# A transformer decoder layer on one core: idle products, an earlier bias product, roots before masked picks and bf16 mask rows in its first rounds

## What is computed

```python
x = x + self_attention(layernorm(x), W_qkv)          # causal, scale 1/sqrt(128)
q, k, v = layernorm(x) @ Wq.T + bq, ctx @ Wk.T + bk, ctx @ Wv.T + bv    # 16 heads of 8
scores = where(mask == 0, -1e9, q @ k.T / sqrt(8))   # mask: 32 x 1 x 128, int32
x = x + (softmax(scores) @ v) @ Wo.T + bo
g, u = qdq(h @ Wg.T), qdq(h @ Wu.T)                  # h = qdq(layernorm(x)), qdq: 16-bit levels
x = x + qdq(qdq(g * u16(sigmoid(g))) * u) @ Wd.T
```

## Time and profile before

| what | us |
|---|---|
| median of three runs (332.31 to 333.15) | 332.85 |
| the profiled execution | 332.82 |
| its span, first to last instruction | 331.0 |
| TensorE busy | 304.9 (92%) |
| VectorE busy | 273.5 (83%) |
| ScalarE busy | 255.1 (77%) |
| GpSimd busy | 192.1 (58%) |
| DMA, mean over the span | 69 GB/s |

### The profile page before, as it was taken

The page is one execution under the profiler, slowest core; times in us unless marked ns, Lnnn a source line. Parts: engine busy times, 40 slices in busy tenths (PEclk is TensorE's granted clock), DMA queues, the critical chain, the costliest instruction groups (busy, mean ns, idle before and its releaser), DMA issues.

```text
span 331.0 us, 9933 instructions
## 1 busy us (share of the span) xinstructions
PE 304.9 (92%) x3741; PEld 208.7 (63%) x3741; DVE 273.5 (83%) x652; ACT 255.1 (77%) x470; POOL 192.1 (58%) x339
## 2 busy tenths in 40 slices
PE   2899999999999999999999999999978689697996
PEld 1587877877656666666666665854423244357996
DVE  5349998878979999999999984877789996989754
ACT  3258988887789989989988987787797768993940
POOL 3467999984238698768658578200067773781000
PEclk9999999999999999999999999999997999999999
DMA  6891336672011556500000000000000000000134
GB/s 155 248 300 35 96 110 184 190 219 95 30 42 49 176 160 191 170 4 5 3 5 2 4 5 2 1 0 0 2 0 0 1 1 2 0 0 1 34 95 128
DMA packets 23755, 22.70 MB, mean 69 GB/s; under 512 B 3546, under 2 KB 21403, under 8 KB 23579
## 3 DMA queue, kind: packets, MB, share of 16 engines
q1 hardware_dynamic: 22170, 21.78, 21.4%
q10 hardware_dynamic: 1536, 0.28, 0.5%
HBM read 15.75 MB, written 6.31 MB: 67 GB/s over the span
## 4 chain that ended last, share of the span: by engine, by line
PE 65%; DVE 12%; ACT 8%; POOL 7%; issue 4%; DMA 2%; SPq 1%; POOLq 0%; ACTq 0%; DVEq 0%
PE banks L763 11%; PE banks L707 9%; PE banks L989 8%; DVE mxs L1820 7%; PE banks L1059 7%; PE banks L637 5%; PE banks L785 4%; PE banks L776 3%; PE banks L630 3%; ACT ng L1355 2%; PE banks L781 2%; PE banks L716 2%; POOL rstd L380 2%; PE banks L649 2%; PE banks L971 2%
## 5 line engine op out<-in xcount | busy, mean ns | idle before, releaser
L1594 DVE TENSOR_REDUCE nm<-banks 128x4 f32<-128x512 f32 x128 | 83.1, 682 | 7.2 <-PE banks L707 5.8
L1258 ACT ACTIVATE PT<-banks,bmask,vmask 128x1024 f32<-128x1024 f32 x64 | 76.6, 1199 | 0.0
L989 PE MATMUL banks<-X3T,upT 128*128 128x512 f32 x96 | 45.9, 620 | 9.9 <-DVE mxs L1820 7.3
L576 POOL TENSOR_TENSOR G<-ng,sq 128x1536 int32<-128x1536 int32 (+3 forms) x10 | 27.9, 2790 | 36.4 <-DVE sq L1851 36.4
L1820 DVE TENSOR_REDUCE mxs<-G 128x1 f32<-128x1536 int32 (+3 forms) x30 | 42.2, 1425 | 4.3 <-ACT G L1316 3.8
L763 PE MATMUL banks<-PT,VP 128*32 128x128 f32 x1024 | 41.2, 279 | 0.0
L989 PEld LDWEIGHTS banks<-X3T,upT 128*128 128x128 f32 x96 | 17.7, 196 | 33.8 <-issue 16.3
L707 PE MATMUL banks<-kd,qd 32*128 32x128 f16 x512 | 37.9, 217 | 1.1 <-ACT pT L1130 0.7
L1100 ACT ACTIVATE h<-X,shift,rstd 128x128 f32<-128x128 f32 x64 | 26.3, 483 | 10.2 <-POOL shift L425 10.1
L707 PEld LDWEIGHTS banks<-kd,qd 32*128 32x128 f16 x512 | 22.7, 92 | 17.7 <-DVE nm L1594 7.2
L763 PEld LDWEIGHTS banks<-PT,VP 128*32 128x32 f32 x1024 | 24.1, 109 | 9.8 <-issue 3.0
(11 more groups left out here) (200 smaller groups left out, 744.4 us busy)
## 6 DMA issues: line engine op xcount, KB each, us to landing
kd<-k_dram SPq DMA_DIRECT2D x32, 128.0 KB, 2.7
qd<-q_dram SPq DMA_DIRECT2D x32, 128.0 KB, 2.8
ctxg<-in_ctx_dram SPq DMA_DIRECT2D x8, 256.0 KB, 3.1
X3T<-m_dram SPq DMA_DIRECT2D x1, 1792.0 KB, 10.2
out_dram<-y SPq DMA_DIRECT2D x7, 256.0 KB, 2.3
X<-in_x_dram SPq DMA_DIRECT2D x3, 512.0 KB, 10.0
k_dram<-khi SPq DMA_DIRECT2D x7, 128.0 KB, 1.9
k_dram<-klo SPq DMA_DIRECT2D x7, 128.0 KB, 1.9
```

Of the source, the lines that this page charges most:

```text
L576: nc.gpsimd.tensor_tensor(GI[:, c], ng[:, u, part], sq[:, u, part], ALU.mult).then_inc(S["b_t"], 1)
L989: m = pe.matmul(bank(2 + FC * (g % 2) + k), w[:, k * P:k * P + P], grp(X3T, g), start=True, stop=True)
L1258: act.activation(PT[:, a, :], bank(2 + 2 * a, 2), ACT.Exp, bias=bmask[:, n:n + 1], scale=vmask[:, n:n + 1]).then_inc(S["t_exp"], 1)
L1594: V.tensor_reduce(nm[:, n % 2, c:c + NSET], bank(u).rearrange("p (h m) -> p h m", m=P), AX.X, ALU.max, negate=True).then_inc(S["t_max"], 1)
```

## The change

Seven edits. TensorE issues unit products (identity times identity, into bank 4) at three places ahead of the first group: five, one and two. `output_bias` comes ahead of the wait for the causal mask and `scores1(0)`. In rounds 1 and 2 GpSimd's `scale_and_shift` comes ahead of `pick_masked`; from round 3 on the order is as before. `MR`, `m_dram` and `mrow` are bf16 instead of f32. The second-but-one block of x (groups 2 and 3) is loaded ahead of the biases of v and o instead of behind the first mask rows. The large load of mask rows comes ahead of the feed-forward weights instead of behind them.

```diff
-        MR = sb("MR", [B, P], where=early)
+        MR = sb("MR", [B, P], BF16, where=early)
-        mrow = X3T
+        mrow = X3T[:, :].bitcast(BF16)
-        m_dram = dram("m_dram", [B, P], F32)
+        m_dram = dram("m_dram", [B, P], BF16)
@@ sync
             sp.dma_start(m_dram, MR[:, :]).then_inc(S["m_st"], 16)
+            load_x(slice(2 * GB, B // 2), "ld_x2")
...
             sp.dma_start(mrow[:, 0:GT], flat[0:GT].partition_broadcast(P)).then_inc(S["ld_mr0"], 16)
-            load_x(slice(2 * GB, B // 2), "ld_x2")
+            sp.dma_start(mrow[:, GT:B * P], flat[GT:B * P].partition_broadcast(P)).then_inc(S["ld_mr"], 16)
             for n, w in enumerate((w_gate, w_up)):
...
-            sp.dma_start(mrow[:, GT:B * P], flat[GT:B * P].partition_broadcast(P)).then_inc(S["ld_mr"], 16)
@@ gpsimd
-                if live(i - 1):
+                if i > 2:
                     pick_masked(i - 1)
-                if live(i):
-                    scale_and_shift(0, i, "s_agg", "s_h", "s_var", "s_pow", "s_neg", "s_rstd")
+                scale_and_shift(0, i, "s_agg", "s_h", "s_var", "s_pow", "s_neg", "s_rstd")
+                if 0 < i < 3:
+                    pick_masked(i - 1)
@@ tensor
+            def idle_products(n, k):
+
+                for _ in range(k):
+                    pe.matmul(bank(n)[:, 0:P], ident[:, :], ident[:, :], start=True, stop=True)
+
             pe.wait_ge(S["c_id"], 1)
+            idle_products(4, 5)
             pe.wait_ge(S["ld_ws"], 16)
...
             pe.transpose(bank(5)[:, P:2 * P], WS[:, P:2 * P], ident[:, :]).then_inc(S["w_t1"], 1)
+            idle_products(4, 1)
...
             pe.matmul(bank(5)[:, 3 * P:3 * P + B], ones[:, :], vmask[:, :], start=True, stop=True).then_inc(S["m_cnt"], 1)
+            idle_products(4, 2)
...
                 if i == 1:
+                    output_bias()
                     pe.wait_ge(S["c_wz"], 6)
                 if live(i - 1):
                     scores1(i - 1)
-                if i == 1:
-                    output_bias()
```

More of the change, by code:

```diff
@@ L966, in _ @@
             turn_rows3(6, NG - 2)
-            def idle_products(n, k):
-                for _ in range(k):
-                    pe.matmul(bank(n)[:, 0:P], ident[:, :], ident[:, :], start=True, stop=True)
             def over_partitions(n, where):
```

## The result

The changed kernel takes 330.62 us (median of 22 runs, 328.91 to 333.08) against 332.51 us before (22 runs, 331.73 to 333.28): a ratio of 0.9937, with a 95% interval of 0.9921 to 0.9953. That is 1.9 us faster, inside the range, by half of the 4.0 us that were forecast. The profiled execution took 329.18 us (span 327.4) against 332.82 us, 3.6 us less; it is one of the faster ones of its kernel. The spread of the changed kernel is 4.2 us, nearly three times that of the kernel before (1.6 us). The mean granted clock of each run tells where part of it comes from: nine of the 22 runs had 0.999 or 1.000, with a median of 329.7 us, and thirteen had 0.99 to 0.995, with a median of 331.0 us. One stretch of 3.4 us at half the clock takes 0.005 off the mean.

What follows compares the result with a forecast made beforehand. Taken to bound it: TensorE at its low clock to about 21.6 us, then GpSimd's unbroken conveyor. 3.8 us off the chain plus 0.2 us for bf16 make 4.0 us, from 332.85 to 328.8 us; range 327.8 to 331.8.

Steps and rivals of the forecast that it cites:

- the landmarks: Start of the kernel: weighted values of group 0 end near 20 us, GpSimd's first second-norm root starts near 23.2 us.
- bf16's share: GpSimd's masked picks with bf16 mask rows: 0.2 us of gain taken, from -0.6 to +3.1 us possible.
- the sum: First groups step by step: scores end 14.1, exponentials wait for ScalarE's rows, weighted values end 20.1 instead of 24.05 us.
- The cause of the early clock: TensorE's start: unit products raise the clock to 2.4 GHz at 11 us instead of about 21.6 us.
- the prediction's own last sentence: Prediction is wrong if unit products don't raise the clock, or if the conveyor's period of some 9 us changes.
- The conveyor passes everything on: GpSimd's unbroken work, 27.15 to 50.64 us: whatever reaches it earlier moves it and all that hangs on it equally.
- R3: Later stages, to the head-wise scores, keep half of the gain: 330.8 us, chance 0.12.
- Little is late next: After the faster start: context 1 is asked for at 17.3 instead of 21.6 us, its user comes near 23.
- R1: TensorE's start: the clock rises only near 15 us, gain 3.0 us, 329.8 us, chance 0.20.
- R4: Before the first scores: late bias loads make TensorE wait for c_bcol, +2 us, 334.5 us, chance 0.05.
- R5: GpSimd's masked picks: bf16 costs a conversion pass, 5 x 0.61 us lost of 4, 332 us, chance 0.04.

## Why the prediction was right where it was, and wrong where it wasn't

- **The time.** 330.62 us lies in the stated range, but not in the forecast's own (328.0 to 329.6). The range reaches that far only because it takes in the rivals, so the hit is theirs and partly luck: the gain at the start was right and half of it didn't reach the end.
- **The start.** Right within 0.3 us at the landmarks: 4.0 us were worked out at the weighted values, 4.1 us were measured, and 4.4 us at 60 us with bf16's share. The steps between were not as worked out. The clock rose between 13 and 14 us and not at 11, the scores ended at 15.1 us (14.1), and the exponentials waited for the maxima, to 15.88 us, which the sum had ruled out. In the sum the finished exponentials (16.8 us) wait for TensorE until 17.3; in the trace they came at 17.4. This slack took up the delay, and that is luck.
- **The cause of the early clock.** Not borne out, and by the prediction's own last sentence a sign that it is wrong. The prediction let the unit products raise the clock. By the durations, five profiles of the new order without products or with weak or few ones show rises near 12, 12, 12, 17 and 17 us; six with the eight full products lie at 11 to 14 us; the kernel before is near 21.6 us, with two key buffers too, and near 12 us with the products alone. It looks as if the new order brought the rise forward, but that isn't shown. In the profile of two key buffers without products the rise falls inside L656, which took 1.64 us instead of 2.04. Up to there TensorE had run the same instructions as in the kernel before, at the same times within 0.12 us; the bias product comes behind. In times no worth of the products is shown with two buffers, and with one they may cost up to about 1 us (328.7 against 329.7 us, intervals that overlap). What sets the moment in a single execution stays open.
- **The conveyor passes everything on.** This sentence failed. It holds to the head-wise scores and not through them. R3 named the waits there and argued them away: "these are issued by the work itself, so they move too". They do move, but with one key buffer the landing had grown by 0.8 to 1.3 us, with an instruction load in its time that the products' own 32 instructions had moved there, and the clock falls behind the longer hole in some executions. R3's 330.8 us is close to the 330.62 measured. It had been given 0.12. The term that was missing is the price of added instructions far from where they stand.
- **Loads.** The sum took bf16 at 0.2 us and the wait for the mask rows as their use. Undone they cost 3.4 us: GpSimd waited 2.28 us for the mask rows, three times the 0.7 us that the experiment's expectation had, and context 1 is next in the queue. "Little is late next" was true of the changed kernel only because of this part; the prediction didn't price what the faster start would have met without it.
- **Rivals.** R1's time of the rise (15 us and later) did occur among the variants. R4 didn't: c_bcol was made at 11.88 us, behind 512 KB of x. R5 didn't: L399 1.16 us. The mask's store, with pieces of 256 B, landed in 2.5 us (2.7 before). Over the ten profiles with bf16 rows it took 2.5 to 3.6 us, over the four with f32 rows 2.5 to 2.8 us. By the Trainium skill's rule on pieces under 512 B ("DMA: Bandwidth & Descriptors", Specifications) they cost a read-modify-write; the traces leave room for a price of up to 1.1 us in some executions and don't part it from the load of x that is now issued right behind it. In the profile of the changed kernel nothing waited for it. The Trainium skill's rule that transposes don't count for the clock as products do ("TensorE: Matmul & The Clock Gate", Part 4: PE-mode transpose) is neither shown nor refuted.
- **Slips in the sums.** R4's +2 us on 332.85 is 334.85, not 334.5. The chances add up to 0.86 for faster and 0.09 for no change, not 0.82 and 0.13. Neither moves the forecast.

## What to carry to other kernels

When a stage is made faster, follow the lead to the next place where an engine waits for a transfer: a single buffer that is refilled there takes the lead back, and a second buffer was worth more (2.6 us) than most parts of this change. On the kernel before it was worth 0.8 us. Fill TensorE's holes only where it is late itself: where it then waits for another engine, a faster clock makes a longer hole, and the clock can fall. Added instructions aren't free because they fit in a gap, since they move the loads of later instructions; look for an instruction load inside each transfer on the chain.

## What the runs showed of the hardware

- One 16 KB load of instructions (queue q8) in the time of a 128 KB store made it land in 3.31 to 3.83 us instead of 2.3 to 2.6 us, in eight profiles against six, with no exception for this store. The 128 KB store issued half a microsecond ahead of it landed in 2.3 to 2.6 us in all fourteen, so a load in the time of a store doesn't delay it by itself. What the load and the late store share was not tested.
- In the first 90 us TensorE's granted clock fell after holes of 1.75, 2.17, 2.29 and 3.70 us, to 1.2 GHz for 3.4 us in three of the cases and about 7 us in the last, and held after holes of 1.57, 1.65 and 1.76 us. Near 250 us all fourteen profiles have the same hole of 2.07 us in the same work; the clock fell behind it in five and held in nine. So the length of a hole doesn't decide alone.
- The fall near 250 us cost nothing: with it (profile of two key buffers) the products of that stage (L989 of the kernel before) took 45.8 us and the waits ahead of them 9.9 us, without it (changed kernel) 44.3 and 11.5 us. The fall ahead of the head-wise scores went with 1.3 us (6.2 us against 7.6 us to the split of the maxima).
- In the profile of two key buffers it was high at 5.87 us already (L617 in 0.49 us instead of 0.80) and low again from about 8.5 to 12 us, with no hole over 0.92 us before it. While low it was shown as such in the profile's windows; before its first rise the windows show 1.00 and only the durations tell.
- But for that one, the first rise came at 11 to 17 us in eleven executions of nearly equal kernels (near 21.6 us in the two with the order before and no products), and at 12 and 17 us in two whose first 12 us of TensorE are the same program. So a single profile of a kernel's start shows one draw.
- GpSimd's product with a bf16 operand took 1.16 us against 1.27 us with f32.
